# Causal scores in 32x32 tiles, keys expanded four-fold, two score stages four steps apart, values projected later

## Chip, cores and metric

The kernel runs on one core of one Trainium2 chip. The metric is the device time of one execution in microseconds; the median of three runs of the kernel before is 1314.33 us (1312.63 to 1318.47). Engines are named as in the profile: PE (TensorE matmul; PEld is its weight load), DVE (VectorE), ACT (ScalarE), POOL (GpSimd), SP (the queue that issues the DMAs).

## Reference

Input x is [32, 256, 128] (batch, tokens, channels), float32, layer-normalised first. The result is x plus two branches: a self-attention over the 256 tokens (covariance scores, 16 heads of 8 channels), and a block in which the batch of 32 is the sequence: a causal attention over 32 positions for each of the 256 tokens, then eight experts of which two are chosen per row.

```python
xn = layernorm(x)
x = x + attn(xn, Wq, Wk, Wv, Wo) + ffn(xn, ...)

def ffn(x, ...):                         # s = 32 positions, b = 256 tokens, 16 heads of 8
    qkv = layernorm(x, ln1) @ in_proj_w.T + in_proj_b
    scores = einsum('sbnd,tbnd->bnst', q, k) / sqrt(8)
    scores = where(tril, scores, -inf)
    attn = einsum('bnst,tbnd->sbnd', softmax(scores), v) @ out_proj_w.T + out_proj_b
    x1 = x + attn
    hn2 = layernorm(x1, ln2)
    gates = top-2 of softmax(hn2 @ router_w.T)
    hmid = gelu(hn2 @ w1[e])             # 8 experts, 256 hidden
    return x1 + sum_e gates[e] * (hmid @ w2[e])
```

## The kernel before

The work has two halves. In the first, 32 attention steps run, one for each batch entry, each of 16 head slots; their result z goes to DRAM. In the second, the 256 tokens are taken in 16 groups of 16 tokens; with 32 positions each that is 512 rows (TOK), held as four tiles (TILES) of 128 rows, a tile being four tokens (QUAD) of 32 positions (SEQ). Every engine runs its own in-order program, and semaphores alone tie them.

A group passes through three stages, and one group step (`group_step`, lines 828, 1227, 1441, 1539) works on three groups at once: the experts of group g (`expert_up`, `expert_down`, `hidden`, `add_expert`), the tail of group g+1 (block transposes, `causal_pv`, normalisation, `causal_out`, `make_x1`, `h2_transposes`, `router_logits`, `choose`, `make_gates`), and the head of group g+2 (`hn_transposes`, `causal_q`, `causal_k`, `causal_v`, `expand_k`, `causal_scores`, `score_maxima`, `causal_exp`); the statistics and normalisation of group g+3 run too. A step has 16 places u (expert e = u // 2, half c = u % 2). At each u PE does one `expert_up` (three f16 matmuls), then what the table `PE_G` (line 42) puts there, then at odd u `expert_down(e - 1)`; the last down follows u = 15. DVE adds expert e - 1 at odd u, then does what `DVE_G` (line 44) puts there, in the order of the code in its step; ACT does one Gelu (`hidden`), then what `ACT_G` (line 46) says. The tables `PE_FIRST`, `DVE_FIRST`, `ACT_FIRST` (49 to 52) place the head of group 0 by head slots of the last attention steps, slot 0 being the first head of attention step 31.

The steps of the head, by lines:
- `hn_transposes` (619) writes the transposed normalised rows into the head bank (misc[0], or bank[0] for group 0) and waits for `s_gxh` and, since `take_v` reads the same bank, for `s_vexp` of the group before (625). `hn_out` (1340, ACT) copies it to hnT.
- `causal_q` (630), `take_q` (981, DVE), `causal_k` (634) use that bank one after the other. `expand_k` (1347, ACT) makes Kexp: for each of 16 heads a copy of all keys, zeroed outside that head's 8 channels by the scale `head_mask` and the bias `head_bias`: 16 activations of 128x512 in eight pieces (k0 to k7).
- `causal_v` (638) projects the values into the same bank; `take_v` (987, DVE) copies them into Vexp in four copies of 32 partitions.
- `causal_scores(n, t)` (644): for tile t the causal mask is put into a score bank by one bf16 matmul, then four f32 matmuls (K = 128, 32 columns of queries, 512 columns of Kexp) add the scores. Tiles 0 and 1 wait for the two score banks to be free (`s_son`), tiles 2 and 3 for the maxima of the tile before last.
- `score_maxima` (997, DVE) reduces and subtracts; `causal_exp` (1358, ACT) runs at the end of the step.

The tail: `block_transposes` (1127), `causal_pv` (770), `causal_normalise` (1135), `merged_transposes`, `causal_out` (790), `make_x1` (1148, x1 and its statistics), POOL's `scales2` (434), `normalise_x1` (1167), `h2_transposes`, `h2_out`, `split_hn2` (1118), `router_logits`, `choose` (1176). DVE's `group_normalise` (963) makes gxh and gxb. `prepare` (1070, DVE) runs once near the start.

Of the kernel before, what the change touches and what calls it, by code (L numbers as in the profile page):

```python
# [6 lines left out]
BF16 = mybir.dt.bfloat16  # L7
# [6 lines left out]
P = 128  # L14
NB, NS, E = 32, 256, 128
H = 16
# [24 lines left out]

PE_G = dict(hn=0, q=2, k=4, v=12, pv=4, scores0=14, scores1=14, scores2=15, scores3=15, merge=6, out=9,
            h2=12, router=14)
DVE_G = dict(spT=2, q=1, seq_out=3, x1=8, h2=8, v=11, split=12, max0=14, max1=14, max2=14, max3=14,
             choose=14, statistics=7, normalise=14)
ACT_G = dict(hn=0, k0=3, k1=4, k2=5, k3=5, k4=7, k5=7, k6=9, k7=10, merged=7, h2=12)


PE_FIRST = dict(hn=0, q=3, k=5, v=15, scores0=16, scores1=17, scores2=18, scores3=19)
DVE_FIRST = dict(statistics0=-6, normalise0=-1, q=4, statistics1=8, normalise1=14, v=16,  # L50
                 max0=17, max1=18, max2=19, max3=20)
# [16 lines left out]
def positive(count):  # L68

    return not isinstance(count, int) or count > 0  # L70
# [59 lines left out]
def attention_and_experts_kernel(nc, x, Wq, Wk, Wv, Wo, ln1_w, ln1_b, in_w_t, in_b, out_w_t, out_b,  # L130
                                 ln2_w, ln2_b, router_t, w1, w2, out):
    ctx = ExitStack()
    with ctx:
        def sb(name, shape, dt=F32):
            return ctx.enter_context(nc.sbuf_tensor(name, shape, dt))
# [19 lines left out]
        def score_bank(n, t):  # L155
            return bank[1 + t % 2] if isinstance(n, int) and n == 0 else seq_bank[t % 2]
# [53 lines left out]
        head_mask = sb("head_mask", [P, H])  # L210
        head_bias = sb("head_bias", [P, H])
        seq_eye = sb("seq_eye", [SEQ, QUAD, SEQ], BF16)
        causal = sb("causal", [SEQ, H, SEQ], BF16)
        index8 = sb("index8", [P, TILES, NE])
# [13 lines left out]

        Kexp = sb("Kexp", [P, GPOS, H, SEQ])

        Vexp = sb("Vexp", [P, TILES, H, QUAD, FEAT])
        smax = sb("smax", [P, TILES, H])

# [131 lines left out]
        def _(pool):  # L365
# [87 lines left out]
            def masks():  # L453
# [10 lines left out]
                pool.wait_ge(s_pool, own.next())  # L464
                pool.memset(seq_eye[:], 0.0).then_inc(s_pool, 1)
                pool.wait_ge(s_pool, own.next())
                pool.affine_select(out=seq_eye[:], in_=seq_eye[:], compare_op=ALU.not_equal, fill=1.0,
                                   base=0, pattern=[[0, QUAD], [-1, SEQ]], channel_multiplier=1).then_inc(s_pool, 1)
                pool.wait_ge(s_pool, own.next())
                pool.memset(causal[:], 0.0).then_inc(s_pool, 1)  # L470
                pool.wait_ge(s_pool, own.next())
                pool.affine_select(out=causal[:], in_=causal[:], compare_op=ALU.is_ge, fill=MASKED,
                                   base=0, pattern=[[0, H], [-1, SEQ]], channel_multiplier=1).then_inc(s_pool, 1)
# [35 lines left out]
        def _(pe):  # L509
# [133 lines left out]

            def causal_scores(n, t):
                if t < 2:
                    if positive(2 * (n - 1) + t + 1):
                        pe.wait_ge(s_son, 2 * (n - 1) + t + 1)
                else:
                    pe.wait_ge(s_sdiff, 4 * n + t - 1)
                m = score_bank(n, t)  # L650
                mm(m[:], seq_eye[:].rearrange("k n s -> k (n s)"), causal[:].rearrange("k h t -> k (h t)"),
                   stop=False)
                for q in range(QUAD):
                    c = t * P + q * SEQ
# [89 lines left out]
            def first_head(b, h):  # L744
                slot = first_slot(b, h)
                if slot == PE_FIRST["hn"]:
                    hn_transposes(0)
                if slot == PE_FIRST["q"]:
                    causal_q(0)
                if slot == PE_FIRST["k"]:  # L750
                    causal_k(0)
                if slot == PE_FIRST["v"]:
                    causal_v(0)
                for t in range(TILES):
                    if slot == PE_FIRST[f"scores{t}"]:
                        causal_scores(0, t)

# [70 lines left out]
            def group_step(g, p):  # L828
                ffn, tail, head, norm = group_present(g)
                for u in range(FC * NE):  # L830
# [11 lines left out]
                    if u == PE_G["pv"] and tail:  # L842
                        causal_pv(g + 1)
                    for t in range(TILES):
                        if u == PE_G[f"scores{t}"] and head:
                            causal_scores(g + 2, t)
                    if u == PE_G["merge"] and tail:
# [16 lines left out]
        def _(dve):  # L864
# [205 lines left out]
            def prepare():  # L1070
# [196 lines left out]
        def _(act):  # L1267
# [131 lines left out]
            def first_head(b, h):  # L1399
                slot = first_slot(b, h)  # L1400
                if slot == ACT_FIRST["hn"]:
                    act.wait_ge(s_setup, 4)
                    hn_out(0)
                for i in range(H // 2):
                    if slot == ACT_FIRST["k0"] + i:
                        expand_k(0, 2 * i, 2 * i + 2)
# [34 lines left out]
            def group_step(g, p):  # L1441
                ffn, tail, head, norm = group_present(g)
                for u in range(FC * NE):
# [7 lines left out]
                    if u == ACT_G["h2"] and tail:  # L1451
                        h2_out(g + 1)
                    for i in range(H // 2):
                        if u == ACT_G[f"k{i}"] and head:
                            expand_k(g + 2, 2 * i, 2 * i + 2)
                if tail:
# [121 lines left out]
```

## Time and profile before

| | before |
|---|---|
| median of three runs | 1314.33 us |
| span of the profiled execution | 1312.0 us |
| PE busy | 1219.3 us (93%) |
| DVE busy | 1059.6 us (81%) |
| ACT busy | 960.6 us (73%) |
| POOL busy | 312.5 us (24%) |
| chain that ended last | PE 62%, ACT 18%, issue 9%, DVE 8% |

The profile is one execution. Its page gives the busy time of each engine, groups of instructions with the idle time in front of them, and the chain that ended last. The trace behind it gives timelines (start, duration, engine, line, what is written from what, how many, and in brackets the idle time ahead with what ended it) and busy time by stretches. Matmuls are pipelined: one starts before the displayed end of the last, so the cost of a group of matmuls is read from start to start.

### The profile page before, as it was taken

The numbers are of one execution on the slowest core, as the hardware profiler recorded it, in microseconds if no ns is written. First come the engines' busy times: TensorE is split into PE (matmuls) and PEld (weight loads), VectorE is DVE, ScalarE is ACT, GpSimd is POOL, SyncE is SP. The second block draws the span as 40 slices with busy tenths as digits, with TensorE's granted clock in tenths as the row PEclk, the third lists the DMA queues.
The fourth block names the chain that finished last, engine by engine and source line by source line (L and its number), as shares of the span: only waits on it lengthen the run. The fifth ranks groups of instructions, "written<-read, shape, count | busy, mean of one in ns | idle before, by whom it ended". The sixth has DMA issues, their size and how long they took to land.

```text
span 1312.0 us, 35299 instructions
## 1 busy us (share of the span) xinstructions
PE 1219.3 (93%) x12100; PEld 783.7 (60%) x12100; DVE 1059.6 (81%) x3074; ACT 960.6 (73%) x1696; POOL 312.5 (24%) x510
## 2 busy tenths in 40 slices
PE   2699999999999999999768999999999999999998
PEld 1456666555656566565335666676666676666676
DVE  5888888888888888888457887888887888887873
ACT  1388898888888898888756667776667776667744
POOL 4334433343333433341120111110111110111000
PEclk9899999999999999999869999999999999999999
DMA  3000000000000000000010000000000000000000
GB/s 94 5 15 15 14 17 17 17 13 13 17 17 13 13 17 17 17 14 15 17 29 17 26 10 17 24 24 24 24 8 16 24 24 24 24 4 20 17 10 16
DMA packets 50855, 24.93 MB, mean 19 GB/s; under 512 B 6384, under 2 KB 50288, under 8 KB 50800
## 3 DMA queue, kind: packets, MB, share of 16 engines
q1 hardware_dynamic: 50800, 24.21, 6.6%
q8 instruction: 33, 0.54, 0.2%
q14 instruction: 22, 0.18, 0.0%
HBM read 15.28 MB, written 8.39 MB: 18 GB/s over the span
## 4 chain that ended last, share of the span: by engine, by line
PE 62%; ACT 18%; issue 9%; DVE 8%; ACTq 1%; DMA 1%; SPq 1%; POOL 1%; DVEq 0%; POOLq 0%
PE bank L515 54%; ACT Kexp L1353 6%; PE bank L546 4%; ACT hmid L1438 4%; ACT prob L1331 3%; DVE smax L1002 2%; PE bank L596 2%; ACT prob L1364 1%; DVE prob L1006 1%; ACT KT L1322 1%; PE bank L615 1%; DMA x_in<-in_L_attn_x 1%; ACT oT L1272 1%; ACT feat L1286 1%; DVE Vexp L994 1%
## 5 line engine op out<-in xcount | busy, mean ns | idle before, releaser
L924 DVE TENSOR_REDUCE rowmax<-bank 128x2 f32<-128x512 f32 x512 | 336.7, 685 | 59.5 <-PE bank L515 56.3
L1331 ACT ACTIVATE prob<-bank 128x512 f32<-128x512 f32 x512 | 294.0, 601 | 29.2 <-PE bank L515 24.6
L515 PEld LDWEIGHTS bank<-w_sb,hmid 128*128 128x128 f32 x2048 | 244.0, 192 | 23.7 <-issue 11.7
L1438 ACT ACTIVATE hmid<-bank,up_scale 128x512 f32<-128x512 f32 x256 | 176.2, 733 | 110.1 <-PE bank L515 109.9
L515 PE MATMUL bank<-w_sb,hmid 128*128 128x128 f32 x2048 | 248.2, 276 | 0.0
L1353 ACT ACTIVATE Kexp<-bank,head_bias,head_mask 128x512 f32<-128x512 f32 x256 | 188.2, 848 | 42.5 <-PE bank L515 42.5
L515 PE MATMUL bank<-QT,KT 128*128 128x256 bf16 x1024 | 197.3, 275 | 10.2 <-ACT prob L1331 7.1
L515 PE MATMUL bank<-KT,QT 128*128 128x256 bf16 x1024 | 200.4, 279 | 5.7 <-DVE rowmax L924 5.1
L1222 DVE SCALAR_TENSOR_TENSOR acc<-bank,gate,acc 128x128 f32<-128x128 f32 x512 | 143.3, 342 | 72.3 <-PE bank L515 70.2
L515 PE MATMUL bank<-prob,V 128*9 128x256 f32 x2048 | 159.6, 384 | 0.0
L1322 ACT COPY KT<-bank 64x1024 bf16<-64x1024 bf16 x128 | 128.8, 1007 | 27.6 <-PE bank L546 23.1
L515 PEld LDWEIGHTS bank<-KT,QT 128*128 128x128 bf16 x1024 | 78.0, 98 | 112.6 <-issue 54.8
L436 POOL TENSOR_TENSOR rstd<-mv,epsilon 128x4 f32<-128x4 f32 x16 | 8.9, 554 | 503.1 <-DVE mv L1160 503.1
L515 PEld LDWEIGHTS bank<-QT,KT 128*128 128x128 bf16 x1024 | 89.1, 98 | 44.2 <-ACT prob L1331 17.4
L515 PE MATMUL bank<-hn_hi,w_lo 128*128 128x512 f16 x256 | 98.0, 383 | 8.9 <-ACT hmid L1438 7.4
L515 PE MATMUL bank<-hn_lo,w_hi 128*128 128x512 f16 x256 | 97.5, 381 | 0.0
L515 PE MATMUL bank<-hn_hi,w_hi 128*128 128x512 f16 x256 | 97.5, 381 | 0.0
L546 PE MATMUL bank<-identb,stack 128*128 128x128 bf16 x1024 | 75.8, 224 | 10.6 <-DVE stack L902 5.2
L546 PEld LDWEIGHTS bank<-identb,stack 128*128 128x128 bf16 x1024 | 62.9, 100 | 33.4 <-issue 14.2
L381 POOL TENSOR_TENSOR rstd<-mv,epsilon 128x2 f32<-128x2 f32 x32 | 6.2, 195 | 264.3 <-DVE mv L885 264.3
L515 PE MATMUL bank<-Kexp,gqT 128*32 128x512 f32 x512 | 68.9, 611 | 0.0
L515 PEld LDWEIGHTS bank<-prob,V 128*9 128x9 f32 x2048 | 30.5, 88 | 54.8 <-issue 48.4
(164 smaller groups left out, 1846.6 us busy)
## 6 DMA issues: line engine op xcount, KB each, us to landing
x_in<-in_L_attn_x SPq DMA_DIRECT2D x32, 128.0 KB, 2.1
QT<-shiftT SPq DMA_DIRECT2D x256, 2.0 KB
z_scratch<-z_out SPq DMA_DIRECT2D x32, 128.0 KB, 1.8
xg<-in_L_attn_x SPq DMA_DIRECT2D x64, 64.0 KB, 1.9
zg<-z_scratch SPq DMA_DIRECT2D x64, 64.0 KB, 2.0
out<-acc SPq DMA_DIRECT2D x64, 64.0 KB, 1.7
w_sb<-in_L_ffn_w SPq DMA_DIRECT2D x1, 1024.0 KB, 6.8
in_wT<-in_L_ffn_in_proj_w SPq DMA_DIRECT2D x1, 192.0 KB, 2.4
```

What stands on the lines that cost most here:

```text
L515: return pe.matmul(o, l, r, start=start, stop=stop, skip_group_check=True)
L546: ins = pe.transpose(m[:, q * NS + st * P:q * NS + (st + 1) * P], stack[:, a, st, h:h + 2, :].rearrange("p h k -> p (h k)"), identb[:])
L596: ins = pe.transpose(misc[0][:, c:c + P], oT[k][:, g, st * P:(st + 1) * P], ident[:])
L615: ins = pe.transpose(misc16(1)[0:SROWS, st * P:(st + 1) * P], shift[k][:, st].rearrange("p a r q -> p (a r q)"), identb[:])
L924: dve.tensor_reduce(rowmax[h // 8][:, :, h % 2, h % 8 // 2], row_scores[h % 3][:].rearrange("p (s t) -> p s t", s=ST), AX.X, ALU.max).then ...
L994: ins = dve.tensor_copy(Vexp[rows, :, :, q, 0:D], ps[rows])
L1002: dve.tensor_reduce(smax[:, t, :], ps, AX.X, ALU.max).then_inc(s_dve, 1)
L1222: ins = dve.scalar_tensor_tensor(out=acc[p][:, t, :], in0=down_bank[e % 2][:, t * P:(t + 1) * P], scalar=gate[p][:, t, e:e + 1], in1=acc[p ...
L1322: ins = act.copy(KT[p][a][rows, half, :], ps[rows])
L1331: act.activation(prob[:, h % 8].rearrange("p t s -> p (t s)"), col_scores[h % 2][:], ACT.Exp, scale=1.0 / D).then_inc(s_exp, 1)
L1353: ins = act.activation(Kexp[:, :, h, :], head_bank(n)[:].rearrange("p (n t) -> p n t", n=GPOS), ACT.Identity, bias=head_bias[:, h:h + 1], ...
L1438: act.activation(hmid[e % 2][c][:], up_bank[c][:], ACT.Gelu, scale=up_scale[:, 0:1]).then_inc(s_mid, 1)
```

## The change

Keys are expanded four-fold: Kexp holds for each token four copies, in copy j only the channels of heads j, 4+j, 8+j and 12+j. The scores of four heads (row group r = head // 4, partitions 32r to 32r+31) then come from 32x32 tiles: 32 rows of queries and keys, 32 columns of queries, 128 columns of Kexp, and score bank r holds heads 4r to 4r+3 of all four tiles instead of one tile with all heads. `causal_scores(n, k)` does two banks (row groups 2k and 2k+1) in turn: two masks, then 32 matmuls that alternate between the two row groups. There are two such stages in a step, at u = 8 and u = 12, with their maxima at the same u on DVE. The mask and its identity are needed on all partitions and are copied by DVE in `prepare`. `expand_k(n, j)` is one activation, four in all. The values are projected at u = 14 instead of 12 and copied at u = 15 instead of 11; hn moves from u = 0 to 1 on PE, x1 from 8 to 9, h2 from 8 to 10, split from 12 to 13, statistics from 7 to 6 on DVE. All waits that are not shown stay as they are.

```diff
-PE_G = dict(hn=0, q=2, k=4, v=12, pv=4, scores0=14, scores1=14, scores2=15, scores3=15, merge=6, out=9,
+PE_G = dict(hn=1, q=2, k=4, v=14, pv=4, scores0=8, scores1=12, merge=6, out=9,
             h2=12, router=14)
-DVE_G = dict(spT=2, q=1, seq_out=3, x1=8, h2=8, v=11, split=12, max0=14, max1=14, max2=14, max3=14,
-             choose=14, statistics=7, normalise=14)
-ACT_G = dict(hn=0, k0=3, k1=4, k2=5, k3=5, k4=7, k5=7, k6=9, k7=10, merged=7, h2=12)
+DVE_G = dict(spT=2, q=1, seq_out=3, x1=9, h2=10, v=15, split=13, max0=8, max1=8, max2=12, max3=12,
+             choose=14, statistics=6, normalise=14)
+ACT_G = dict(hn=0, k0=4, k1=5, k2=5, k3=6, merged=7, h2=12)
...
-PE_FIRST = dict(hn=0, q=3, k=5, v=15, scores0=16, scores1=17, scores2=18, scores3=19)
-DVE_FIRST = dict(statistics0=-6, normalise0=-1, q=4, statistics1=8, normalise1=14, v=16,
+PE_FIRST = dict(hn=0, q=3, k=5, v=11, scores0=16, scores1=17)
+DVE_FIRST = dict(statistics0=-6, normalise0=-1, q=4, statistics1=8, normalise1=14, v=12,
                  max0=17, max1=18, max2=19, max3=20)
...
-            def causal_scores(n, t):
-                if t < 2:
-                    if positive(2 * (n - 1) + t + 1):
-                        pe.wait_ge(s_son, 2 * (n - 1) + t + 1)
+            def causal_scores(n, k):
+
+                if k == 0:
+                    pe.wait_ge(s_kexp, n + 1)
+                    if positive(2 * n):
+                        pe.wait_ge(s_son, 2 * n)
                 else:
-                    pe.wait_ge(s_sdiff, 4 * n + t - 1)
-                m = score_bank(n, t)
-                mm(m[:], seq_eye[:].rearrange("k n s -> k (n s)"), causal[:].rearrange("k h t -> k (h t)"),
-                   stop=False)
-                for q in range(QUAD):
-                    c = t * P + q * SEQ
-                    ins = mm(m[q * SEQ:(q + 1) * SEQ, :], gqT[:, c:c + SEQ],
-                             Kexp[:, t * QUAD + q].rearrange("p h t -> p (h t)"), start=False)
-                ins.then_inc(s_sc, 1)
+                    pe.wait_ge(s_sdiff, 4 * n + 2)
+                for r in (2 * k, 2 * k + 1):
+                    rows = slice(r * SEQ, (r + 1) * SEQ)
+                    mm(score_bank(n, r)[:], seq_eye[rows].rearrange("k q s -> k (q s)"),
+                       causal[rows].rearrange("k h t -> k (h t)"), stop=False)
+                for t in range(TILES):
+                    for q in range(QUAD):
+                        c = t * P + q * SEQ
+                        for r in (2 * k, 2 * k + 1):
+                            rows = slice(r * SEQ, (r + 1) * SEQ)
+                            ins = mm(score_bank(n, r)[q * SEQ:(q + 1) * SEQ, t * P:(t + 1) * P],
+                                     gqT[rows, c:c + SEQ],
+                                     Kexp[rows, t * QUAD + q].rearrange("p j t -> p (j t)"), start=False)
+                            if t == TILES - 1 and q == QUAD - 1:
+                                ins.then_inc(s_sc, 1)
...
-                                 sprobT[:, t, h, :], Vexp[:, t, h].rearrange("p n c -> p (n c)"))
+                                 sprobT[:, h // QUAD, QUAD * t + h % QUAD, :],
+                                 Vexp[:, t, h].rearrange("p n c -> p (n c)"))
...
-                dve.tensor_scalar(head_bias[:], head_mask[:], in_bT[:, 1:2], None, ALU.mult)
+                for r in range(1, QUAD):
+                    dve.tensor_copy(causal[r * SEQ:(r + 1) * SEQ], causal[0:SEQ])
+                    dve.tensor_copy(seq_eye[r * SEQ:(r + 1) * SEQ], seq_eye[0:SEQ])
+                dve.tensor_reduce(quad_mask[:], head_mask[:].rearrange("p (r j) -> p j r", r=QUAD), AX.X,
+                                  ALU.add).then_inc(s_dve, 1)
+                dve.wait_ge(s_dve, own.next())
+                dve.tensor_scalar(head_bias[:], quad_mask[:], in_bT[:, 1:2], None, ALU.mult)
...
-            def expand_k(n, lo, hi):
-                if lo == 0:
+            def expand_k(n, j):
+                if j == 0:
                     act.wait_ge(s_gk_ps, n + 1)
                     if positive(4 * n):
                         act.wait_ge(s_sc, 4 * n)
-                for h in range(lo, hi):
-                    ins = act.activation(Kexp[:, :, h, :], head_bank(n)[:].rearrange("p (n t) -> p n t", n=GPOS),
-                                         ACT.Identity, bias=head_bias[:, h:h + 1], scale=head_mask[:, h:h + 1])
-                if hi == H:
+                ins = act.activation(Kexp[:, :, j, :], head_bank(n)[:].rearrange("p (n t) -> p n t", n=GPOS),
+                                     ACT.Identity, bias=head_bias[:, j:j + 1], scale=quad_mask[:, j:j + 1])
+                if j == QUAD - 1:
                     ins.then_inc(s_kexp, 1)
```

## Rows read from the trace of the kernel before

**Rows 1.** The page's costliest groups: busy us, mean ns, idle before.
```profile
L1353 ACT ACTIVATE Kexp<-bank,head_bias,head_mask 128x512 f32<-128x512 f32 x256 | 188.2, 848 | 42.5 <-PE bank L515 42.5
```

**Rows 2.** Busy time by stretches: one step; then PE, PEld, DVE, ACT, POOL, clock.
```profile
738.90:778.40 39.50, 38.38 (x382) 26.03 (x380) 32.62 (x115) 27.36 (x43) 5.82 (x10) 1.00 0.08 22
```

**Rows 3.** Timeline of PE, one group step: start us, duration us, what, count [idle before].
```profile
905.29 1.33 PE L515 MATMUL bank<-Vexp,sprobT 128*32 128x36 f32 x128 [0.23 <-DVE sprobT L1132]
906.56 0.39 PE L515 MATMUL bank<-hn_hi,w_lo 128*128 128x512 f16 x1
...
907.22 1.95 PE L515 MATMUL bank<-w_sb,hmid 128*128 128x128 f32 x16
909.00 0.38 PE L515 MATMUL bank<-hn_hi,w_lo 128*128 128x512 f16 x1
...
913.81 1.05 PE L515 MATMUL bank<-out_wT,aT 128*128 128x128 f32 x8
914.70 1.95 PE L515 MATMUL bank<-w_sb,hmid 128*128 128x128 f32 x16
...
925.20 0.39 PE L515 MATMUL bank<-causal,seq_eye 32*128 32x512 bf16 x1
925.52 1.06 PE L515 MATMUL bank<-Kexp,gqT 128*32 128x512 f32 x8
926.51 0.39 PE L515 MATMUL bank<-causal,seq_eye 32*128 32x512 bf16 x1
...
937.08 0.66 PE L627 MATMUL bank<-ident,gxh 128*128 128x128 f32 x4 [0.49 <-DVE gxh L968]
...
938.83 0.39 PE L515 MATMUL bank<-hn_hi,w_lo 128*128 128x512 f16 x1 [0.45 <-ACT hmid L1438]
```

**Rows 4.** Timeline of DVE, same step, and x1 eight steps later.
```profile
914.96 0.66 DVE L1152 TENSOR_TENSOR x<-bank,gxb 128x512 f32<-128x512 f32 x1
...
918.70 1.12 DVE L1172 TENSOR_SCALAR h2n<-x,mv,rstd 128x128 f32<-128x128 f32 x4 [1.19 <-POOL rstd L438]
...
922.00 2.78 DVE L994 COPY Vexp<-bank 32x512 f32<-32x512 f32 x4
924.81 0.48 DVE L1122 TENSOR_SCALAR hn_hi<-hn2T,hn_scale 128x512 f16<-128x512 f32 x1
...
926.12 1.12 DVE L1222 SCALAR_TENSOR_TENSOR acc<-bank,gate,acc 128x128 f32<-128x128 f32 x4
...
932.26 0.68 DVE L1002 TENSOR_REDUCE smax<-bank 128x16 f32<-128x512 f32 x1
...
933.58 0.18 DVE L1179 COPY logit<-bank 128x32 f32<-128x32 f32 x1
...
935.91 1.12 DVE L968 TENSOR_SCALAR gxh<-xg,gmv,gr 128x128 f32<-128x128 f32 x4 [0.20 <-DVE pick L1200]
...
938.70 1.12 DVE L1222 SCALAR_TENSOR_TENSOR acc<-bank,gate,acc 128x128 f32<-128x128 f32 x4
...
1230.86 0.69 DVE L1152 TENSOR_TENSOR x<-bank,gxb 128x512 f32<-128x512 f32 x1 [1.06 <-PE bank L515]
```

**Rows 5.** Timelines of ACT and PE between the halves of the kernel.
```profile
637.13 1.44 ACT L1353 ACTIVATE Kexp<-bank,head_bias,head_mask 128x512 f32<-128x512 f32 x2
...
652.09 1.28 ACT L1331 ACTIVATE prob<-bank 128x512 f32<-128x512 f32 x2
...
699.27 1.11 PE L627 MATMUL bank<-ident,gxh 128*128 128x128 f32 x4 [3.98 <-DVE gxh L968]
...
703.59 0.38 PE L515 MATMUL bank<-hn_hi,w_lo 128*128 128x512 f16 x1
```

**Rows 6.** Timeline of PE at two other waits.
```profile
644.87 0.61 PE L515 MATMUL bank<-QT,KT 128*128 128x256 bf16 x2 [1.43 <-ACT prob L1331]
...
1254.83 0.39 PE L515 MATMUL bank<-hn_hi,w_lo 128*128 128x512 f16 x1 [1.55 <-ACT hmid L1438]
```

**Rows 7.** Timeline of DVE near the start.
```profile
25.88 1.14 DVE L902 COPY stack<-stack 128x576 bf16<-128x576 bf16 x2
```

More of the change, by code:

```diff
@@ L210, in attention_and_experts_kernel @@
         head_mask = sb("head_mask", [P, H])
-        head_bias = sb("head_bias", [P, H])
-        seq_eye = sb("seq_eye", [SEQ, QUAD, SEQ], BF16)
-        causal = sb("causal", [SEQ, H, SEQ], BF16)
+        head_bias = sb("head_bias", [P, QUAD])
+        quad_mask = sb("quad_mask", [P, QUAD])
+        seq_eye = sb("seq_eye", [P, QUAD, SEQ], BF16)
+        causal = sb("causal", [P, H, SEQ], BF16)
         index8 = sb("index8", [P, TILES, NE])
@@ L227, in attention_and_experts_kernel @@
         gqT = sb("gqT", [P, TOK])
-        Kexp = sb("Kexp", [P, GPOS, H, SEQ])
+        Kexp = sb("Kexp", [P, GPOS, QUAD, SEQ])
         Vexp = sb("Vexp", [P, TILES, H, QUAD, FEAT])
-        smax = sb("smax", [P, TILES, H])
+        smax = sb("smax", [P, QUAD, H])
         sdiff = prob[:, 0:4].rearrange("p t s (h k) -> p t (s h) k", k=SEQ)
@@ L464, in masks @@
                 pool.wait_ge(s_pool, own.next())
-                pool.memset(seq_eye[:], 0.0).then_inc(s_pool, 1)
+                pool.memset(seq_eye[0:SEQ], 0.0).then_inc(s_pool, 1)
                 pool.wait_ge(s_pool, own.next())
-                pool.affine_select(out=seq_eye[:], in_=seq_eye[:], compare_op=ALU.not_equal, fill=1.0,
+                pool.affine_select(out=seq_eye[0:SEQ], in_=seq_eye[0:SEQ], compare_op=ALU.not_equal, fill=1.0,
                                    base=0, pattern=[[0, QUAD], [-1, SEQ]], channel_multiplier=1).then_inc(s_pool, 1)
                 pool.wait_ge(s_pool, own.next())
-                pool.memset(causal[:], 0.0).then_inc(s_pool, 1)
+                pool.memset(causal[0:SEQ], 0.0).then_inc(s_pool, 1)
                 pool.wait_ge(s_pool, own.next())
-                pool.affine_select(out=causal[:], in_=causal[:], compare_op=ALU.is_ge, fill=MASKED,
+                pool.affine_select(out=causal[0:SEQ], in_=causal[0:SEQ], compare_op=ALU.is_ge, fill=MASKED,
                                    base=0, pattern=[[0, H], [-1, SEQ]], channel_multiplier=1).then_inc(s_pool, 1)
@@ L753, in first_head @@
                     causal_v(0)
-                for t in range(TILES):
-                    if slot == PE_FIRST[f"scores{t}"]:
-                        causal_scores(0, t)
+                for k in range(2):
+                    if slot == PE_FIRST[f"scores{k}"]:
+                        causal_scores(0, k)
             def prepare():
@@ L843, in group_step @@
                         causal_pv(g + 1)
-                    for t in range(TILES):
-                        if u == PE_G[f"scores{t}"] and head:
-                            causal_scores(g + 2, t)
+                    for k in range(2):
+                        if u == PE_G[f"scores{k}"] and head:
+                            causal_scores(g + 2, k)
                     if u == PE_G["merge"] and tail:
@@ L1403, in first_head @@
                     hn_out(0)
-                for i in range(H // 2):
-                    if slot == ACT_FIRST["k0"] + i:
-                        expand_k(0, 2 * i, 2 * i + 2)
+                for j in range(QUAD):
+                    if slot == ACT_FIRST["k0"] + j:
+                        expand_k(0, j)
                 for t in range(TILES):
@@ L1452, in group_step @@
                         h2_out(g + 1)
-                    for i in range(H // 2):
-                        if u == ACT_G[f"k{i}"] and head:
-                            expand_k(g + 2, 2 * i, 2 * i + 2)
+                    for j in range(QUAD):
+                        if u == ACT_G[f"k{j}"] and head:
+                            expand_k(g + 2, j)
                 if tail:
```

## Prediction

> **What bounds the kernel now.** I read the page's costliest groups first: ACT spends 188.2 us on expanding the keys [rows 1]. That looks like a large gift, until the second half of the kernel is read by stretches: in one group step of 39.5 us PE is busy 38.4 us, DVE 32.6 and ACT 27.4 [rows 2]. ACT has 12 us to spare there, so what it saves is not time. Next the timelines of PE and DVE over one step. PE runs without pause except at one place, around the transposes of gxh (I call them hn): 0.49 us idle until DVE has gxh, then 0.45 us until ACT has the first hmid [rows 3]. The wait before hn is short, but it closes a loop: hn at 937.08; x1 of the next step at 914.96 + 39.5 = 954.46, so 17.4 us later; then DVE works almost without a gap from x1 at 914.96 to the end of gxh at 937.03 [rows 4], 22.1 us. 17.4 + 22.1 is the whole period, and the x1 of two steps eight apart confirm it: (1230.86 - 914.96)/8 = 39.5 us [rows 4]. So PE and DVE bound a step in turn, and a step costs the PE work from hn to x1 plus the DVE work from x1 to whatever hn waits for. That is what the change must be priced against.
>
> **Part 1: the score matmuls.** A stage costs now 925.20 to 926.51 = 1.31 us: 0.32 for the mask and 1.0 for four f32 matmuls of 512 columns in four column tiles [rows 3]. Four stages are 5.25 us. The new pair of stages has the same four column tiles times two row tiles and a quarter of the columns per matmul. That row tiles run beside each other no row shows. Low: all eight at once, each four matmuls of 128 columns, which is half the stream of two old stages, so 1.0 us, plus one mask's 0.32 if the masks overlap too, less a little: 1.2. High: row tiles take turns, as two old stages, 2.6. I take 1.5 per pair (1.0 of stream, two masks nearly in turn), since the column tiles do overlap in [rows 3]. The Trainium skill (TensorEngine Tiling (Array Packing), Key Properties) says that tiles operate independently and may load and multiply in parallel; by it the pair would be at the low end, 1.2 to 1.5; the trace has that for column tiles alone.
>
> **Part 2: key expansion.** 12 of 16 activations per group go, 0.72 us each [rows 5], 8.7 us of ACT. In the steady steps I cost that at nothing: the cover is ACT's 12 us of idle time [rows 2]. ACT still has its Exps between choose and the first hmid, and this fits (the 0.45 us wait of [rows 3] goes, since PE will be waiting longer elsewhere).
>
> **Part 3: the moves, where the time is decided.** hn of the next group overwrites the bank from which take_v copies the values, and therefore waits for s_vexp. Until now take_v ran at DVE's step 11, far ahead of hn. Now v is projected at PE's step 14 and copied at DVE's step 15, behind choose, the whole normalisation and an expert's addition; hn stands at step 1 of the next step. So hn waits for take_v, and PE's later ups and downs, the hmid of ACT and take_q queue behind hn.
> - From hn to x1 (PE). From the up behind hn, 938.83, to the next out, 913.81 + 39.5, are now 14.48 us [rows 3]. New: hn 0.49, then that 14.48 less the 0.23 us wait for sprobT, plus 0.3 because q now stands one up closer to hn and waits for ACT's copy of hnT (about as long as one Kexp, 0.72 [rows 5], against an up of 0.65), plus 1.6 for the pair of scores at step 8 with its switch. out starts 16.7 after hn. x1 now stands behind add_expert(3), which needs the down of step 9: out 0.89, down 1.78 (907.22 to 909.00), 0.2 latency, addition 1.04 (1.12 less its overlap) [rows 3, 4]. x1 starts 20.6 us after hn, 3.2 later than now. DVE's own work in that time is about 14 us (32.6 [rows 2] less the 18.4 that the other part keeps it busy), so PE sets it.
> - From x1 to the end of take_v (DVE) [rows 4]: x1 to h2n 3.74 (with POOL's rstd inside), h2n 1.03 (1.12 less the overlap), addition 1.04, two maxima 2 x 1.32 (932.26 to 933.58 is one), addition 1.04, split 1.31, choose 2.33, gxh and gxb with bias 2.79, addition 1.04, take_v 2.81 (922.00 to 924.81). Sum 19.8 us. The way to hn is 2.3 us shorter than the old 22.1 (two maxima and one wait are out of it), but hn came later by more.
> - Period: 20.6 + 19.8 = 40.4 us against 39.5.
> - PE's wait: from the end of down 3 PE needs about 17.2 us to reach hn (seven ups 4.55, downs 4 to 7 at 1.78 each with 0.1 between, pair 1.6, the rest v, router, h2 and a wait of h2 for h2n); DVE reaches the end of take_v 0.2 + 1.04 + 19.8 = 21.0 us after it. PE idles 3.8 us before hn in every step; now it is 0.5.
>
> **Part 4: the clock.** After 3.98 us idle before one hn, [rows 5] show the transposes at 1.11 us instead of 0.66 [rows 3]: the granted clock fell to the lower level of 1.2 GHz. It has also fallen after a nearly idle stretch with 1.43 us idle before the matmul at 644.87 (0.61 instead of 0.38 us), but not after 1.55 us at 1254.83, where work was dense before [rows 6]. The predicted wait lies next to the 3.98. There PE was back at the upper level before 703.59 [rows 5], so some 3.4 us went at half rate, 1.7 us lost, of which ACT's copy of hnT, which q waits for anyway, would hide 0.4 here. A step loses 1.3 us then; bounds 0 and 1.7. I take 1.0, since it may not fall each time. Period 41.4.
>
> **Part 5: what occurs once.** Start: DVE makes three copies of causal (32x512 bf16, near the 128x576 bf16 copies at 1.14/2 us [rows 7]), three of seq_eye and a reduction ahead of the weights' scaling, which is on the chain: +1.5 us (0.8 to 2.5). Transition: in the last attention step Kexp sits between Exps on ACT from 637.13 to 652.09 [rows 5] and sets the pace; 12 x 0.72 = 8.7 us go, but take_v and the normalisation of group 1 (5.6 us of DVE) then come into the way of the maxima: I take -6.9 (-4 to -9). The step without experts: Kexp goes here too, but the same chain through x1 to take_v stands in its place: +0.3 (-4 to +3). End: the last step with a head is followed by no hn; from its own hn to its last down PE needs 20.6 - 1.2 to the end of down 3 and 15.9 behind it, 35.4 us, against 38.2 now (39.5 less the 1.3 of an up and a wait before hn), -2.8, and the 1.7 us wait for hmid before 1254.83 [rows 6] goes; the first without scores waits for h2n (+2.3), as nothing fills PE ahead of h2, and for sprobT (+1.3): -1 (-3 to +1).
>
> **Sum.** 13 periods lie between the hn of groups 2 and 15. 13 x (41.4 - 39.5) = +24.7; +1.5 - 6.9 + 0.3 - 1.0 = -6.1; together +18.6. On the span of the profiled execution, 1312.0, that is 1330.6; the median of the runs is 2.3 us above this span, so 1333.
>
> **Rivals.**
> 1. The clock holds: period 40.4, 13 x 0.9 - 6.1 = +5.6, 1320. For it: 1254.83 in [rows 6]. Against: 3.98 us did lower it. The Trainium skill (TensorE: Matmul & The Clock Gate, What's actually happening) calls the throttled state the default that activity releases; by that it falls, as forecast.
> 2. Row tiles take turns: pair 2.6, period 41.5, and PE's wait shrinks to 2.9 us, so with 0.8 for the clock 42.3: 13 x 2.8 - 6 = +30, 1345.
> 3. Tiles serialise wholly, each change of row tile draining the column tiles: 64 matmul instructions of 128 columns at 0.11 us (eight in 0.89 at out [rows 3]) are 7 us a pair. Then the second pair too lies on the way, and the period is near 51: about 1460. Only total absence of overlap does this.
> 4. The other side, faster: DVE is not what hn waits for. If the chain from x1 to take_v took 16.0 us or less instead of 19.8, PE would bound the step: 39.5 less today's waits of 1.8 and the 2.1 saved on scores is 35.6, with 0.9 of new small waits a period of 36.5, 13 x -3 - 6 = -45, 1269. This decides at those 16.0 us. For it: ACT's 8.7 us and PE's 2.3 us are truly gone. Against: each of the chain's terms is a measured row, and nothing in it is removed.
> 5. The change does what it says, but all one-time terms and the pair fall at their good ends, clock held: period 40.1, 13 x 0.6 - 12 = -4, 1310.
>
> **How the numbers follow.** Forecast 0.52, rival 1 0.18, rival 2 0.12, rival 3 0.04, rival 4 0.06, rival 5 0.08. A measurement of this kernel tells about 0.5% from no change, 6.6 us: same is 1308 to 1321. Slower: forecast, 2, 3 and a quarter of 1, less what the forecast loses at its lower edge: 0.71. Same: most of 1 and 5: 0.22. Faster 0.07. The range takes in rivals 1, 2 and 5: 1310 to 1350.
>
> **What would show it.** PE idle before hn (released by DVE Vexp) near 3.8 us, 14 times; its transposes at 1.1 us where the clock fell; x1 20.6 us behind hn; end of take_v 19.8 behind x1; the score pair 1.5 us; Kexp at 64 activations with no effect inside a step; DVE still near 33 us busy a step. Wrong if hn does not wait for Vexp, if a pair takes 3 us or more, or if the last attention step does not shorten.

## The result, and the profile after

The changed kernel takes 1349.83 us (median of four runs, 1349.24 to 1351.4) beside 1314.48 us for the kernel before on the same chip: an estimated ratio of 1.0273, 95% interval [1.0254, 1.0292]. That it would be slower was forecast, and the sum (+18.6 us) was about half of what came. The profiled executions differ by 1347.5 - 1312.0 = 35.5 us, and that difference is explained below.

From the page after (totals, the clock in 40 slices, the queue that brings instructions, the chain that ended last), then the key expansion from the full list of groups:

```profile
PE 1201.0 (89%) x13636; PEld 814.8 (60%) x13636; DVE 1063.3 (79%) x3081; ACT 844.3 (63%) x1504; POOL 312.5 (23%) x510
...
PEclk9899999999999999999669999989888998889899
...
q8 instruction: 88, 1.44, 0.5%
...
PE 66%; DVE 16%; issue 8%; ACT 6%; POOL 2%; DMA 1%; SPq 1%; ACTq 0%; DVEq 0%; POOLq 0%
```
```profile
L1368 ACT ACTIVATE Kexp<-bank,head_bias,quad_mask 128x512 f32<-128x512 f32 x64 | 47.7, 774 | 7.5 <-PE bank L516 7.5
```

Beside [rows 1], the key expansion takes ACT 140 us less (188.2 to 47.7; ACT's busy time in all fell from 960.6 to 844.3), and the kernel became slower. PE is busy for 18 us less in a span that is 35 us longer, and DVE's share of the chain that ended last doubled. Two things are new. The clock line has eights in the second half where the same line of before has nines throughout. And q8, the queue that brings instructions, moved 88 packets; before it was 33.

By stretches, two steps in a row (columns as in [rows 2]):

```profile
906.94:947.67 40.73, 35.94 (x477) 27.43 (x476) 31.08 (x107) 21.14 (x32) 5.82 (x10) 0.96 0.08 21
947.67:991.83 44.16, 38.81 (x477) 28.70 (x477) 34.51 (x122) 19.17 (x29) 5.83 (x10) 0.89 0.08 20
```

The steps are of two lengths, which before they were not, and the granted clock is 0.96 and 0.89 where [rows 2] have 1.00. PE now runs 477 matmul instructions a step, against 382. The timeline of PE around the two hn that bound the first of these steps answers to [rows 3]:

```profile
897.79 1.95 PE L516 MATMUL bank<-w_sb,hmid 128*128 128x128 f32 x16
904.41 0.60 PE L516 MATMUL bank<-hn_hi,w_lo 128*128 128x512 f16 x1 [4.67 <-issue]
...
906.94 1.06 PE L628 MATMUL bank<-ident,gxh 128*128 128x128 f32 x4
...
921.91 0.39 PE L516 MATMUL bank<-causal,seq_eye 32*128 32x512 bf16 x2
922.23 1.15 PE L516 MATMUL bank<-Kexp,gqT 32*32 32x128 f32 x64
923.31 0.39 PE L516 MATMUL bank<-hn_hi,w_lo 128*128 128x512 f16 x1
...
932.83 0.65 PE L809 MATMUL bank<-ident,h2n 128*128 128x128 f32 x4 [0.89 <-DVE h2n L1188]
...
947.67 1.08 PE L628 MATMUL bank<-ident,gxh 128*128 128x128 f32 x4 [3.90 <-DVE Vexp L1004]
948.55 0.63 PE L516 MATMUL bank<-hn_hi,w_lo 128*128 128x512 f16 x1
```

Three things are to be seen. The hn at 947.67 waited 3.90 us for Vexp, as forecast, and from 948.55 a matmul of 512 columns takes 0.43 us from start to start instead of 0.22: the clock is at 1.2 GHz. The pair of scores takes 923.31 - 921.91 = 1.40 us. And the hn at 906.94 waited for nothing, because PE had stood still just before, at 904.41: 4.67 us that ended on "issue", that is, on nothing that another engine delivers. There are five such rows, 4.45 to 5.07 us long, in every second step.

The timeline of DVE in the same step answers to [rows 4]:

```profile
927.89 0.68 DVE L1168 TENSOR_TENSOR x<-bank,gxb 128x512 f32<-128x512 f32 x1
...
944.75 2.78 DVE L1004 COPY Vexp<-bank 32x512 f32<-32x512 f32 x4
947.56 0.18 DVE L1221 TENSOR_REDUCE lsum<-lexp 128x4 f32<-128x32 f32 x1
...
970.25 0.68 DVE L1168 TENSOR_TENSOR x<-bank,gxb 128x512 f32<-128x512 f32 x1
```

x1 starts 927.89 - 906.94 = 20.95 us after hn, and take_v ends 19.7 us after x1 began. In this step the clock was back at the upper level some 1.5 us behind hn. Behind the hn that had waited 3.90 us it came back later, and x1 starts 970.25 - 947.67 = 22.58 us after hn.

**Where the 35.5 us are.** Up to the hn of group 2 the changed kernel is 2.4 us ahead (696.84 against 699.27 in [rows 5]). From there to the hn of group 15 (1245.91; before 1213.56) thirteen periods take 549.1 us against 514.3: +34.8. From that hn to the end it is 101.6 against 98.4: +3.1.

### The profile page after: what moved, and what is told of

Its sections match the earlier page's. It is cut to its first block, busy times and chain, and to the rows that moved or that the text cites. A ratio compares the mean times of both kernels' runs of the same rounds, so it can differ in the third digit from the quotient of the medians.

```text
span 1347.5 us, 38165 instructions
## 1 busy us (share of the span) xinstructions
PE 1201.0 (89%) x13636; PEld 814.8 (60%) x13636; DVE 1063.3 (79%) x3081; ACT 844.3 (63%) x1504; POOL 312.5 (23%) x510
## 4 chain that ended last, share of the span: by engine, by line
PE 66%; DVE 16%; issue 8%; ACT 6%; POOL 2%; DMA 1%; SPq 1%; ACTq 0%; DVEq 0%; POOLq 0%
PE bank L516 56%; PE bank L547 4%; DVE acc L1238 3%; ACT prob L1347 2%; DVE Vexp L1004 2%; PE bank L597 2%; POOL rstd L439 1%; DVE smax L1012 1%; DVE stats L1172 1%; PE bank L628 1%; ACT KT L1338 1%; DVE h2n L1188 1%; DVE gxh L978 1%; DVE gxb L984 1%; PE bank L616 1%
## 5 line engine op out<-in xcount | busy, mean ns | idle before, releaser
L1453 ACT ACTIVATE hmid<-bank,up_scale 128x512 f32<-128x512 f32 x256 | 172.4, 686 | 242.2 <-PE bank L516 242.0
L516 PEld LDWEIGHTS bank<-w_sb,hmid 128*128 128x128 f32 x2048 | 247.3, 193 | 15.3 <-issue 1.9
L516 PE MATMUL bank<-hn_hi,w_lo 128*128 128x512 f16 x256 | 104.8, 409 | 25.8 <-issue 23.6
L516 PE MATMUL bank<-hn_lo,w_hi 128*128 128x512 f16 x256 | 104.5, 408 | 0.0
L516 PE MATMUL bank<-hn_hi,w_hi 128*128 128x512 f16 x256 | 103.8, 405 | 0.0
L1012 DVE TENSOR_REDUCE smax<-bank 128x16 f32<-128x512 f32 x64 | 43.8, 684 | 18.1 <-PE bank L516 18.1
L411 POOL TENSOR_TENSOR stack<-resid,stack 128x288 bf16<-128x288 f32 x64 | 47.3, 759 | 43.6 <-DVE stack L907 43.6
```

What stands on the lines that cost most here:

```text
L411: ins = pool.tensor_tensor(slots[:, a, :, place, :], resid[:, a], slots[:, a, :, 1, :], ALU.subtract)
L516: return pe.matmul(o, l, r, start=start, stop=stop, skip_group_check=True)
L1012: dve.tensor_reduce(smax[:, t, :], ps, AX.X, ALU.max).then_inc(s_dve, 1)
L1453: act.activation(hmid[e % 2][c][:], up_bank[c][:], ACT.Gelu, scale=up_scale[:, 0:1]).then_inc(s_mid, 1)
```

## The experiments

All are timed beside the kernel before, by ratio. Three edits recur. "Unrolled" writes PE's group steps out, so that its program has no jump between them; "early" takes the values back to where they were, and leaves hn and all else as changed; "filled" puts idle matmuls, whose result nobody uses, ahead of hn:

```diff
-            run_groups(pe, group_step)                                  # unrolled
+            for g in range(-1, GROUPS):
+                group_step(g, g % 2)
...
-PE_G = dict(hn=1, q=2, k=4, v=14, ...                                   # early
+PE_G = dict(hn=1, q=2, k=4, v=12, ...
-DVE_G = dict(..., v=15, ...
+DVE_G = dict(..., v=11, ...
...
                     if u == PE_G["hn"] and head:                       # filled
+                        if ffn:
+                            pe.wait_ge(s_sdiff, 4 * (g + 2))
+                            for i in range(FILL):
+                                mm(seq_bank[0][:], w1_hi[:, 0, 0:P], hn2_hi[p][:])
                         hn_transposes(g + 2)
```

**1 and 2: both kernels unrolled.** PE's loop holds two steps and runs six times, so it jumps back five times, and five is the number of "issue" rows.

> The changed kernel with PE's program for the group steps written out step by step instead of as a loop over pairs of steps; nothing else differs. Theory A (PE's loop body has outgrown what PE keeps of its program, so that each jump back has to fetch it again): the five idle stretches of 4.5 to 5.1 us ahead of the first up of every second step, which no semaphore ends, go; the five periods of 44.1 us become 41.1 like the others; 15 us less, about 1335. The Trainium skill (Runtime: NRT & Kernel Launch, Instruction fetch mechanics) says that a taken branch to a page that is not held forces a fetch before execution goes on; by that they go too. Theory B (PE waits there for an engine, and the profile misses the semaphore): the stretches stay, 1350.

> The kernel before with the same writing out of PE's group steps. Theory A: its loop body is still held whole, there are no such stretches to remove, within 3 us of 1314. If writing out helps or harms by itself, this shows by how much; then the gain of the other run is to be corrected by it.

Measured: the changed kernel unrolled 1343.93 us, 1.0211 [1.0188, 1.0234]; the kernel before unrolled 1314.61 us, 0.9997 [0.9986, 1.0007]. The five "issue" rows went (single ones of 0.2 to 0.7 us stand elsewhere in the unrolled programs), and the fourteen hn from group 2 on now all wait for Vexp. From the waits of the first (total us, times, longest):

```profile
PE bank L628 <- DVE Vexp L1005: 55.3, 14, 5.0
```

So the jumps do cost time after the change and none before it, but less than I expected: by ratio 0.0062 x 1314 = 8 us (4 to 12), and between hn 2 and hn 15 of the profiles 549.1 - 540.4 = 8.7 us. I had expected 15 us. The stall lies in front of hn, though, where PE has 3.9 us to wait in any case, so most of its 4.5 to 5.1 us is paid already. The mean period without jumps is 41.57 us.

**3: the idle time before hn filled, so that the clock has no gap to fall in** (unrolled, FILL = 15).

> The changed kernel with PE's group steps written out, and 15 idle matmuls of 512 columns (3.3 us, into a score bank that is free then) ahead of each hn, so that PE is busy while it waits for take_v. The result is not changed by them. Theory A (the lowered clock behind the wait costs about 0.6 us a step, 41.1 against the 40.4 that the chain alone gives): period 40.5, about 8 us less than the written-out one without them, 1327. Theory B (what is slow behind hn is hidden in other waits): no difference to the written-out one, 1335.

Measured: 1323.31 us, 1.0059 [1.0038, 1.008]. The timeline of PE:

```profile
938.11 0.63 PE L629 MATMUL bank<-ident,gxh 128*128 128x128 f32 x4 [0.65 <-DVE Vexp L1010]
```

and of DVE, from x1 on:

```profile
958.55 0.68 DVE L1174 TENSOR_TENSOR x<-bank,gxb 128x512 f32<-128x512 f32 x1
...
975.39 2.78 DVE L1010 COPY Vexp<-bank 32x512 f32<-32x512 f32 x4
```

hn still waits for Vexp, but the transposes take 0.63 us, so the clock held. x1 starts 20.44 us after hn, and take_v ends 19.6 us after x1 began. The period is 40.25 us, the same to 0.1 us in each of twelve steps, and that is the bare chain that was forecast at 40.4. The lowered clock therefore costs 41.57 - 40.25 = 1.3 us a step; by ratio 0.0152 x 1314 = 20 us (16 to 24) in all. I had expected 0.6 us a step and 1327 us. Work that is of no use made the unrolled kernel 1.5% faster.

**4: only the values taken back** (early, with the loop).

> The changed kernel with the values projected at PE's step 12 and copied at DVE's step 11 again; all else as changed. Theory A (hn waits for take_v at the end of DVE's chain): hn then waits for gxh only, 2.8 us of DVE work earlier (gxb with its bias 1.76 and an addition 1.04 drop out of the chain, the copy moves within it), the wait of 3.9 us shrinks to about 1, the period without a jump back falls from 41.1 to about 37.9, and the jumps back now cost their full 4.7 us: 13 x -3.2 + 5 x 1.7 = -33, about 1317. Theory B (the wait for take_v only stands in for another that is as late): the period stays above 40, above 1335.

Measured: 1329.9 us, 1.0098 [1.0068, 1.0128], against 1.0273. The wait for Vexp is gone and five of the steps without a jump take 37.97 us, less than before the change. The steps with one take 43.8 to 45.4 us. Timeline of PE:

```profile
892.43 2.05 PE L516 MATMUL bank<-w_sb,hmid 128*128 128x128 f32 x16 [0.56 <-DVE acc L1238]
899.67 0.61 PE L516 MATMUL bank<-hn_hi,w_lo 128*128 128x512 f16 x1 [5.19 <-issue]
...
940.17 0.66 PE L628 MATMUL bank<-ident,gxh 128*128 128x128 f32 x4 [1.20 <-DVE gxh L978]
```

and two steps, one without a jump and one with it, by stretches (columns as in [rows 2]):

```profile
820.34:858.31 37.97, 36.13 (x478) 27.59 (x476) 28.35 (x98) 19.49 (x31) 5.81 (x10) 0.98 0.08 22
858.31:902.20 43.89, 36.83 (x476) 27.79 (x477) 37.06 (x131) 20.73 (x31) 5.83 (x10) 0.94 0.08 20
```

With no wait to hide behind, the stall costs most of its length: these two steps take 81.86 us together, and two steps without a jump 77.34 (2 x 38.67, run 9). The 37.97 us alone say too little, since DVE does part of that step's work during the stall (28.35 us in it and 37.06 in the other). I had expected 1317 us, with stalls of 4.7 us and all other steps at 37.9. The stalls are 5.0 to 5.5 us, the clock is at the lower level for 6.8 us around each, and the first steps take 40.32 and 38.54 us.

**5: only the values moved, in the kernel before** (hn = 1, v = 14 on PE and 15 on DVE).

> The kernel before with one part of the change alone: hn at PE's step 1, values projected at step 14 and copied at DVE's step 15. Theory A (hn waits for the copy at the end of DVE's chain): from hn to x1 about 16.5 us (17.4 less an up and a wait, plus one for hnT), from x1 to the end of the copy 27.7 us (today's 22.1 to gxh, then gxb 1.76, an addition 1.04, the copy 2.81; today's place of the copy is filled by DVE waiting for scores), with the clock lowered behind each long wait 1.3: period 44 to 45.5, 1375 to 1392. Theory B (the late values matter only together with the early scores): under 1330.

Measured: 1403.95 us, 1.0692 [1.067, 1.0713], above the 1375 to 1392 of theory A; the steps take 45.6 and 46.5 us by turns instead of 44 to 45.5. Each hn from group 2 on waits for Vexp:

```profile
933.25 1.12 PE L627 MATMUL bank<-ident,gxh 128*128 128x128 f32 x4 [5.33 <-DVE Vexp L994]
```

The move (with hn one place later), and nothing else of the change, produces the wait, and a larger one; run 4 took it back and the wait went. So the move is the cause of the wait, and the rest of the change softens it.

**6: only the new scores and keys, at the old places** (unrolled).

```diff
-PE_G = dict(hn=1, q=2, k=4, v=14, pv=4, scores0=8, scores1=12, ...
+PE_G = dict(hn=0, q=2, k=4, v=12, pv=4, scores0=14, scores1=15, ...
-DVE_G = dict(..., x1=9, h2=10, v=15, split=13, max0=8, max1=8, max2=12, max3=12, ..., statistics=6, ...
+DVE_G = dict(..., x1=8, h2=8, v=11, split=12, max0=14, max1=14, max2=14, max3=14, ..., statistics=7, ...
```

> The changed kernel's scores, masks and four-fold keys, but every step in its old place (hn 0, values 12 and 11, scores at 14 and 15, all maxima at 14, x1, h2, split and statistics as before), with PE's group steps written out so that no fetch comes in. Theory A (DVE's chain from x1 to gxh bounds the step, and PE's 2.4 us fewer of scores and ACT's 8.7 us fewer of keys are not on it): period 39.5 to 39.9, 1311 to 1319. Theory B (PE's work bounds the step): 2.4 us less a step, 1283.

Measured: 1336.73 us, 1.0173 [1.0145, 1.0201]. Both expectations missed. The timeline of PE says why:

```profile
894.09 0.60 PE L516 MATMUL bank<-causal,seq_eye 32*128 32x512 bf16 x2 [2.10 <-DVE prob L1017]
894.62 1.96 PE L516 MATMUL bank<-Kexp,gqT 32*32 32x128 f32 x64
896.50 3.68 PE L516 MATMUL bank<-w_sb,hmid 128*128 128x128 f32 x18
```

One new stage, a pair of banks, uses both score banks at once. The second pair must therefore wait until DVE is done with both maxima of the first, where the old single stages took turns with the two banks. PE waits 2.10 us in every step, the clock falls each time for 3.4 or 6.8 us, and 64 matmul instructions take 1.96 us instead of 1.15; a step takes about 41.1 us. At these places the two pairs stand too close together; what did not have to follow, as runs 8 and 9 show, is where the values went.

**7: does the length of the loop's body make the stall?** The kernel before, with its loop, and 96 idle matmuls of one column in each step ahead of hn, which brings it to the changed kernel's 478 instructions.

```diff
+                            for i in range(96):
+                                mm(seq_bank[0][0:1, i:i + 1], w1_hi[:, 0, 0:1], hn2_hi[p][:, 0:1])
```

> The kernel before, still with its loops, and 96 idle one-column matmuls (96 more matmul instructions a step, as many as the change adds) ahead of each hn into a score bank that is free then; the result is not changed. Theory A (the number of PE's instructions in the loop body decides whether a jump back has to fetch): the padding costs about 2.4 us a step where it stands, and besides stretches of about 5 us without a releaser appear ahead of the first up of every second step, five of them: about 1365, with some 50 more packets of instructions. Theory B (the stretches have to do with the 32x32 tiles or the new waits): the padding costs its 2.4 us a step, 1345, no such stretches, 33 packets.

Measured: 1353.63 us, 1.0294 [1.0265, 1.0324], between the two expectations, and the time alone doesn't decide, since the padding itself takes some 2.6 us a step (in its trace 954.17 to 956.95, less 0.22 for a matmul of the up in the same row), and the clock fell too: at nine of the fourteen hn from group 2 on the transposes take 1.1 us. The rows do. From its page and the timeline of PE behind a jump:

```profile
q8 instruction: 86, 1.41, 0.4%
```
```profile
905.40 3.84 PE L515 MATMUL bank<-w_sb,hmid 128*128 128x128 f32 x32
910.89 0.39 PE L515 MATMUL bank<-hn_hi,w_lo 128*128 128x512 f16 x1 [1.65 <-issue]
```

q8 moves 86 packets instead of 33, and five stretches of "issue" of 1.6 to 2.0 us stand behind the five jumps, each with a second one of 0.4 to 1.0 us in the padding that follows. The body's length alone, without the new tiles or waits, brings the packets and the stalls about. Its stalls are shorter than the 4.5 to 5.5 us of the changed kernel, for a reason that I leave open.

The Trainium skill (Runtime: NRT & Kernel Launch, Instruction fetch mechanics) says that a taken branch to a page outside the window held on the engine has to fetch the page before work goes on, and that straight-line code is prefetched. The traces agree as far as they go: the unrolled kernels move more packets than the looped kernel before (63 for it, 75 for the changed one, against 33) and have no stall of that kind, only single "issue" rows of up to 0.9 us. How large the window is they don't show.

**8: values early and unrolled**, both costs taken away.

> The changed kernel with the values early (12 and 11) and PE's group steps written out. Theory A (late values, and the fetch at the jump back, are the two losses; without them the new places are good): all periods 38.0, as the undisturbed ones of the looped run with early values were; 13 x (38.0 - 39.5) = -19.5 on the kernel before, +5 for the last steps, -3 for the transition: about 1297, and faster than both kernels. Theory B (the 5.0 to 5.5 us in front of every second step are not a fetch and come back in another form): 1325 to 1330 as with the loop.

Measured: 1312.85 us, 0.9996 [0.9986, 1.0006], between the two expectations. The 38.0 us a step of theory A came from steps behind a stall; without a jump no step is shorter than 38.6. The steps fall into two kinds, 38.67 and 40.0 us, though their waits are the same; the timeline of PE at two hn in a row:

```profile
932.59 0.66 PE L628 MATMUL bank<-ident,gxh 128*128 128x128 f32 x4 [1.14 <-DVE gxh L979]
934.35 0.39 PE L516 MATMUL bank<-hn_hi,w_lo 128*128 128x512 f16 x1 [1.10 <-ACT hmid L1454]
...
968.12 2.02 PE L516 MATMUL bank<-w_sb,hmid 128*128 128x128 f32 x16 [0.66 <-DVE acc L1239]
972.58 0.66 PE L628 MATMUL bank<-ident,gxh 128*128 128x128 f32 x4 [1.14 <-DVE gxh L979]
```

What differs is the granted clock. By stretches, two longer steps and a short one:

```profile
932.59:972.58 39.99, 37.09 (x477) 27.90 (x477) 32.80 (x115) 20.08 (x31) 5.83 (x10) 0.96 0.08 21
972.58:1012.27 39.69, 35.72 (x477) 27.40 (x477) 32.62 (x115) 20.06 (x31) 5.84 (x10) 1.00 0.08 21
1050.94:1089.61 38.67, 35.56 (x476) 27.32 (x476) 32.61 (x115) 20.06 (x31) 5.83 (x10) 1.00 0.08 22
```

From the hn of group 3 on, the trace has a stretch of 3.4 us at the lower level in five of the six longer steps, and none in those of 38.67. The sixth, of 39.69 us, has none either, but 0.85 us on "issue" at 983.78. The clock fell where three waits (0.66, 1.14, 1.10 us) stand close together; they do so in every step, and it did not fall each time.

**9 and 10: the same, with five idle matmuls** ahead of hn (1.1 us, the length of its wait), and with five more behind hn, in which PE otherwise waits for hmid.

> The values early and the steps of TensorE unrolled, as before, and now five idle matmuls of 512 columns (about 1.1 us of stream; their result is not used) ahead of the transposes of gxh, in the place of the 1.14 us wait. Theory A, the lowered clock is what separates the steps of 38.67 us from those of 40.0 us: every step is then near 38.7 us, six steps save 1.3 us each, and the time is about 1305 us (ratio to the kernel before 0.993). Theory B, the steps of 40.0 us are late for another reason and the lowered clock only goes with it: the steps stay at 38.7 and 40.0 us or become 39.3 throughout, and the time stays near 1313 us (ratio 0.999 to 1.001).

> As the kernel with five idle matmuls ahead of the transposes of gxh, and five more right behind them, where TensorE waits about 1.1 us for hmid. Theory A, it is the idle stretch of about 2.2 us in two pieces, one before and one behind the transposes, that lowers the clock, and one filled piece is not enough: this kernel keeps the upper clock in every step and has steps of 38.7 us, about 1305 us, while the kernel with one filled piece still has some steps of 40 us. Theory B, one piece is enough: this kernel equals the one with five idle matmuls, or is up to 4 us slower (0.3 us a step by what the second five delay).

Measured: 1305.91 us, 0.9937 [0.9925, 0.995], and 1304.74 us, 0.9931 [0.9917, 0.9944]. One step of the first, by stretches, and PE's timeline:

```profile
890.89:929.57 38.68, 36.65 (x482) 27.81 (x482) 32.62 (x115) 20.07 (x31) 5.82 (x10) 1.00 0.08 22
```
```profile
929.57 0.66 PE L629 MATMUL bank<-ident,gxh 128*128 128x128 f32 x4
931.33 0.39 PE L517 MATMUL bank<-hn_hi,w_lo 128*128 128x512 f16 x1 [1.10 <-ACT hmid L1459]
```

From the hn of group 3 to that of group 15 the clock stayed at 1.00, and no step took 40 us again (37.7 to 39.3, most of them 38.67). The lowered clock was what separated the two kinds of steps. One filled wait is enough: the second five change nothing that can be told. This is faster than both kernels, by 0.6% against the one before and 3.3% against the changed one. So the rest of the change (the new scores, keys and places, which no run takes apart) is worth about 0.9 us a step (39.56 to 38.67), if the values are copied early, PE's group steps have no jump and the clock is kept. Some of that is given back once at the end, where hmid is waited for 2.85 us and h2n 2.29. Unrolling alone gave the kernel before nothing (run 2), and its clock is at 1.00 in the steps already.

## Why the prediction was half right

The sum was +18.6 us; the profiled executions differ by 35.5. The step that failed is what the sum puts on top of the bare chain. It has PE's new scores by their stream alone, so the stall behind each jump stands in it at nothing and was +8.7 us; the clock is at 1.0 us a step and cost 1.3; and the terms that occur once are at -6.1 us and came to +0.7. Point by point:

| term | forecast | shown |
|---|---|---|
| bare chain, 13 periods | 13 x 0.9 = +11.7 | 13 x (40.25 - 39.56) = +9.0 |
| lowered clock | 13 x 1.0 = +13.0 | 13 x (41.57 - 40.25) = +17.2 |
| stall behind PE's jumps | not in the sum | +8.7 |
| everything that occurs once | -6.1 | +0.7 |
| sum | +18.6 | +35.6 |

The clock is measured here without jumps and the jumps with the clock as it falls; taken away in another order the two would share their 26 us otherwise. That 1349.83 us lies just inside the stated range of 1310 to 1350 is luck: its upper part was for rival 2, which did not come.

**Right: the mechanism and its size.** The loop from hn through x1 to take_v was read from [rows 3, 4] as 20.6 + 19.8 = 40.4 us; with the clock kept (run 3) it is 20.44 + 19.6 and a period of 40.25. PE's wait was forecast at 3.8 us and is 3.9, at nine hn; at the other five the stall stands in its place. That the key expansion is worth nothing inside a step fits (140 us of it went, and no hn from group 2 on waits for ACT), but no run changes the keys alone. The pair of scores was taken at 1.5 us and takes 1.40, so rivals 2 and 3 fall. Rival 4 falls with the 19.7 us, and rivals 1 and 5, which need the clock to hold, with the 0.43 us matmuls behind 947.67.

**Mis-sized: the clock.** It was taken at 1.0 us a step, with bounds of 0 and 1.7: one row of [rows 5] gave 1.3, and 0.3 was taken off because it may not fall each time. It fell in every one of the thirteen periods, in the changed kernel and unrolled, and costs 1.3 on average.

**Missed: the jumps.** The change puts 96 more matmul instructions into each step. I counted their stream (1.4 us instead of 2.6) and never their number as a property of the program. No row of before shows a stall at a jump, and run 2 finds none; q8's 33 packets on the page of before, fewer than the 63 of the same program unrolled, were the only hint, and I did not use them. Runs 1, 2 and 7 show the term.

**Missed: what occurs once**, 6.8 us of the 16.9 that the sum is short.
- The start was forecast at +1.5: DVE's part of `prepare` grew by 1.5 us, as forecast. At the hn of group 0 only 0.4 us of it is left in this profile (630.08, before 629.68); the seven other profiles of programs that start as the changed kernel have this hn at 631.0 to 632.1, and those that start as the kernel before at 628.6 to 630.0, so 0.4 is one low draw.
- The transition was forecast at -6.9 and gave -3.4 (the hn of group 1 is at 662.68, before at 665.73, and 0.4 us had been lost ahead of it). The last attention step did shorten, as it should with 4 key activations instead of 16, but then this came, in the timeline of PE:

```profile
649.08 1.15 PE L516 MATMUL bank<-Kexp,gqT 32*32 32x128 f32 x64
653.92 0.60 PE L516 MATMUL bank<-causal,seq_eye 32*128 32x512 bf16 x2 [3.14 <-DVE prob L1016]
654.46 1.96 PE L516 MATMUL bank<-Kexp,gqT 32*32 32x128 f32 x64
```

The second pair waits for both maxima of the first, which stand behind take_v and the normalisation of group 1 on DVE; then it runs at the lower clock. I had priced DVE's order but not that a pair takes both banks. Run 6 shows the same in every step.
- The step without experts was forecast at +0.3 and gave +0.6 (34.16 us between the hn of groups 1 and 2, before 33.54).
- The end was forecast at -1 and gave +3.1. The wait for hmid that I took away is still there, h2's wait of 2.3 us is there as forecast, the one for sprobT (1.3 us) did not come, and there is another of 1.83 us for h2n in the step ahead, which I didn't count:

```profile
1273.68 0.99 PE L809 MATMUL bank<-ident,h2n 128*128 128x128 f32 x4 [1.83 <-DVE h2n L1188]
1287.83 0.39 PE L516 MATMUL bank<-hn_hi,w_lo 128*128 128x512 f16 x1 [1.54 <-ACT hmid L1453]
1309.04 0.66 PE L809 MATMUL bank<-ident,h2n 128*128 128x128 f32 x4 [2.29 <-DVE h2n L1188]
```

[Rows 6] had the hmid wait at 1.55, where the prediction took away 1.7. The wait is the same to 0.01 us; I take it that ACT's order behind the last h2 sets it, which the change leaves alone, but no run tests that.

The split of the thirteen periods is taken from one profile each. Beside the times: the ratios give 8 us for the jumps, 20 for the clock (it has one-time parts too) and 8 for the rest, 36 together.

## What to carry to other kernels

A producer moved behind a chain of another engine must be priced over the whole loop that it closes, and the gap that it leaves can be paid twice, as here, once as idle time and once as a lower clock behind it; a few idle matmuls in a gap that can't be closed are worth trying. When an edit cuts one instruction into many, count the instructions of each engine's loop and compare the instruction queue's packets: the stream may shrink while the program no longer fits. And ask of every buffer pair whether the new form takes both at once, since what took turns before will then wait.

## What the runs showed of the hardware

- PE waits of 3.9 us in every step, and of 2.1 us (run 6), were followed by 3.4 or 6.8 us at the lower granted clock, 1.2 GHz; the waits of 3.9 us cost 1.3 us a step by it. Three waits of 0.66, 1.14 and 1.10 us close together were followed by 3.4 us of it in some steps and by none in others.
- Sixty-four f32 matmul instructions of 32 rows, 32 columns of weights and 128 columns take 1.08 us from start to the next, 17 ns each. That is 64 x 128 = 8192 columns, where the old stage has 8 x 512 = 4096 in 0.99 us over four column groups [rows 3], so two row groups do work beside each other, as column groups do.
- A loop of two steps with 382 matmul instructions each (and as many weight loads) jumps back at no cost that the trace shows; with 477 or 478 PE stalls 1.6 to 5.5 us at every jump. Where between these the limit lies was not tried, nor why the stall is about three times as long in one kernel as in the other.
- Five idle matmuls of 512 columns, 1.1 us in every step, made the kernel of run 8 0.6% faster (0.9996 to 0.9937).
